# A decoder layer on one core: one step of a scan moved ahead of another, and row statistics of the next batch made during attention

## The chip, the cores and the metric

The kernel runs on one core of a Trainium2 chip. The core has five engines with a queue each, which meet only at semaphores: TensorE (PE; its weight loads are listed as PEld), VectorE (DVE), ScalarE (ACT), GpSimd (POOL), and SyncE (SP), which issues the DMAs. An engine works through its queue in order, and a wait holds up all that stands behind it. The metric is the device time of one execution in microseconds (us). The kernel before takes 4476.42 us (median of three runs, 4476.28 to 4478.08).

## The reference, cut to what matters

All is float32. The input x is 4 batches of 1024 rows of 512 numbers.

```
x = x + mamba_block(layernorm(x))                        # two scans, forward and backward
x = x + cross_attention(layernorm(x), ctx, ctx, mask)    # 16 heads of 32
x = x + moe_attention(layernorm(x))                      # 16 experts of 64

_mamba2:  z, xBC, dt = split(x @ in_proj_w.T)
          scan over rows:  h = h * dA_t + dt_t * x_t * B_t ;  y_t = h . C_t
          y = y + D * x ;  y = y * silu(z) ;  rmsnorm(y) @ out_proj_w.T
cross_attention:  Q, K, V = projections; softmax(Q K^T / sqrt(32), causal, masked) V @ W_o.T + b_o
layernorm:  (x - mean(row)) / sqrt(var(row) + 1e-5)
```

## The kernel before

Four stages follow one another with barriers between them: the forward scan (tiles named `mf_`), the backward scan (`mb_`), the cross attention (`xa_`) and the expert attention (`ff_`). In each stage a generator `order()` lists the steps, and every engine walks the same list and does its own part of each step. The list therefore sets the order within every engine's queue, SyncE's included; no planner stands behind it.

**The scans.** The rows are cut into 32 chunks of 128 (8 for each batch), and a loop counter n runs over slots. In slot n, `mixed` has TensorE make the gate projection z of chunk n+1 in two halves (line 1260) between the products within chunk n (L1241), and ScalarE the tanh of z (L833). `carry` has TensorE make the product of chunk n with the state that came from the chunk before (L1278, the inter-chunk product) and the state's increment (L1284); VectorE scales the first (L1078) and adds the second to the state (L1090). `gate` has VectorE finish silu(z) in two halves, reading z from PSUM (L1066); that frees the two PSUM banks `mf_proj`. In the forward scan the next user of these banks, in even slots up to 26, is `xT`: TensorE transposes two tiles of rows (L1173) for a later group of two chunks. After that come `output`, with the decay matrices (L1293, L1296; they need the bank that the state's increment was in) and the output product (L1309). In the list, `mixed`, `carry`, `gate` follow in this order in every slot; in even slots nothing of VectorE stands between `carry` and `gate`. Before them VectorE does the convolution taps (L940).

**The cross attention.** One batch after the other. `head()`: x of the batch is loaded in two halves of 1 MB into `src` (which also holds the exponentials of the attention, so the load waits for its last transposes); VectorE makes the row statistics of eight tiles of 128 rows (`stats`, one bn_stats each), per half the reciprocal root in a chain of 12 dependent small steps (`ln`), and normalizes the tiles (`xn`). `body()`: each tile is transposed by TensorE (`src` n), copied by ScalarE and split into a high and a low part by VectorE (L1823); eight `kq` steps make Q and K for four groups of four heads each, through DRAM, and `v` the values. Of these, the even ones need tiles 0 to 3 of the source, the odd ones tiles 4 to 7. The low part of the transposed source lies in the memory from which the output product `o` of the batch before reads, so VectorE's part of `src` 0 waits for the last `o`.

The attention proper is 32 tiles, 8 for each group g (i is the tile in the group, n = 8g + i). For each of four heads: scores (L1960, L1961), a row extreme on VectorE (`minima`, L1866), the exponential on ScalarE (L1781), transposes (L1967), copies on VectorE and ScalarE (L1874, L1790), products with V (L1983). After tiles 3 and 7 of a group VectorE scales the result (L1889, L1891), one tile later, and SyncE moves it (`scale`, L1692). At the end of tile 7 of groups 0 and 1, `loads` has SyncE issue the loads of Q and K for group g+2 (L1683): 4 heads, 2 halves, q and k, 3 parts, 48 DMAs of 64 KB.

```
                if now and now[1] == NT - 1 and now[0] + 2 < NHG:
                    yield from loads(now[0] + 2)
```

The eight output steps `o` t (projection on TensorE, residual and bias in the two buffers of `res`: SyncE loads x again (L1698), GpSimd adds the bias (L1728), VectorE adds the product (L1896), SyncE stores (L1705)) begin in the last tiles of a batch; six of them run at the boundary to the next batch, interleaved in the list with that batch's `head()`. `res` t can be loaded when the store of `res` t-2 has landed. Between the first group's result, which is staged in `res`, and `o` 0 these two buffers are unused.

Of the kernel before, what the change touches and what calls it, by code (L numbers as in the profile page):

```python
# [14 lines left out]
P = 128  # L15
# [86 lines left out]
def rsqrt(nc, step, out, x, v, a, scale, eps):  # L102


    step(nc.vector.tensor_scalar(v, x, scale, eps, ALU.mult, ALU.add))
    step(nc.vector.tensor_scalar(out.bitcast(I32), v.bitcast(I32), -0.5, RSQRT_SEED, ALU.mult, ALU.add))
    for _ in range(3):
        step(nc.vector.tensor_tensor(a, out, out, ALU.mult))
        step(nc.vector.scalar_tensor_tensor(a, a, -0.5, v, ALU.mult, ALU.mult))
        step(nc.vector.scalar_tensor_tensor(out, a, 1.5, out, ALU.add, ALU.mult))  # L110


def split_weight(nc, dve, stage, stage_loaded, hi_ready, half_ready, n, hi, lo):
# [153 lines left out]
def mamba_pass(nc, backward, x_in, w_in, conv_w, conv_b, dt_bias, a_log, d_skip, rms_w, w_out, w_proj,  # L267
# [17 lines left out]
    with ExitStack() as ctx:  # L285
# [122 lines left out]
        def order():  # L408

            yield "load", 0  # L410
            if not backward:
                yield "norm", 0
            for e in range(KD):
                yield "weights", e
                if e == 1:
                    yield "params", 0
            if backward:
                yield "load", 1
            yield "raw", 0
            yield "split", 0  # L420
            yield "split", 1
            if not backward:
                yield "xT", 0
                yield "load", 1
            yield "consts", 0
            for e in range(KD, 2 * KD):
                yield "weights", e
            yield "split", 2
            yield "split", 3
            for n in range(-3, N + 1):  # L430
                if not backward and n % 2 == 0 and 0 <= n // 2 + 2 < NGF:
# [24 lines left out]
                if 0 <= n - 1 < N:  # L456
                    yield "square", n - 1
                if n % 2 and 0 <= (n + 3) // 2 < NGF:
                    yield "tanh", (n + 3) // 2
                if -1 <= n < N:  # L460
                    yield "mixed", n
                if 0 <= n < N:
                    yield "carry", n
                if n % 2 and 0 <= (n + 3) // 2 < NGF:
                    yield "product", (n + 3) // 2
                if -1 <= n < N:
                    yield "gate", n
# [904 lines left out]
def cross_attention(nc, x_in, ctx_in, mask_in, wts, bq, bk, bv, bo, out):  # L1372
# [23 lines left out]
        return g * mine.count(mine[at]) + mine[:at].count(mine[at])  # L1396

    NV = sum(by_vector(t, n) for t in range(NT) for n in range(len(PACK[t])))
    kq_dram = [nc.dram_tensor(tag + n + "_dram", (2, D, S), F32).ap() for n in "kq"]
    held = []  # L1400
    with ExitStack() as ctx:
# [66 lines left out]
        resb_ready = sig("resb_ready", NT)  # L1468
        out_ready = sig("out_ready", NT)
        stored = [sig(f"stored{i}", NT // 2, 16) for i in range(2)]  # L1470
        dve_step = sig("dve_step", 2 * (2 + RSQRT_STEPS))
        const_ready, par_loaded, const_dve = sem("const_ready"), sem("par_loaded"), sem("const_dve")
        stage_loaded = [sem(f"stage_loaded{i}") for i in range(2)]
        hi_ready, half_ready, bq_ready = sem("hi_ready"), sem("half_ready"), sem("bq_ready")
# [13 lines left out]
        def loads(g):  # L1488
            for half in range(2):
                for h in range(g * HG, (g + 1) * HG):  # L1490
                    yield "load", (h, "q", half)
                    yield "load", (h, "k", half)

        def body():

# [14 lines left out]
            for n in range(len(TILES) + 1):  # L1510
# [42 lines left out]
                    yield from loads(1)  # L1553
                if now and now[0] == NHG - 1 and now[1] > QT + 1:
                    yield "o", now[1] - QT - 2
            yield "scale", scale.pop()

        def order():
# [10 lines left out]
            for it in range(B):  # L1569
                if it == 0:  # L1570
                    yield "split", 0, 0
                for what, n in body():
                    if it == 0 and what == "load_ctx":
                        yield "split", 0, 1
                        yield "fetch", 0, 2
# [8 lines left out]
                yield "load_x", it + 1, 1  # L1584
                yield "o", it, QT - 1
                yield "load_mask", it + 1, 0
                yield "o", it, QT
                ahead = [n for n in head() if n[0] != "load_x"]
                cut, end = ahead.index(("xn", 0)), ahead.index(("ln", 1)) + 1
                for what, n in ahead[:cut]:  # L1590
                    yield what, it + 1, n
                yield "o", it, QT + 1
                for what, n in ahead[cut:end]:
                    yield what, it + 1, n
                yield "o", it, QT + 2
                for what, n in ahead[end:]:
                    yield what, it + 1, n
                yield "o", it, QT + 3

        def run(batch):  # L1600
# [29 lines left out]

        @block.sync
        def _(sp):
            for s in ctx_loaded + x_loaded + [mask_loaded] + kq_stored + front_loaded + back_loaded + o_moved + res_loaded + stored:
                s.start(sp)
            for t, a in params:
                sp.dma_start(t, a).then_inc(par_loaded, 16)
# [7 lines left out]
            def batch(it):  # L1644
# [49 lines left out]
                def output(t):  # L1694
# [3 lines left out]
                        sp.dma_start(res[:, t % 2, :], x_in[it, t * P:(t + 1) * P, :]).then_inc(res_loaded[t % 2].sem, 16)  # L1698

                    if t == 0:  # L1700
                        load_res(0)
                    if t + 1 < NT:
                        load_res(t + 1)
                    sp.wait_ge(out_ready.sem, out_ready.at(it, t))
                    sp.dma_start(out[it, t * P:(t + 1) * P, :], res[:, t % 2, :]).then_inc(stored[t % 2].sem, 16)  # L1705

                return {"fetch": fetch, "load_mask": mask, "load_x": load_x, "load_ctx": load_ctx, "kq": store, "load": load, "scale": move,
                     "o": output}

            run(batch)  # L1710
# [84 lines left out]

        @block.vector
        def _(dve):
            for s in [mask_ready, xn_ready, slo_ready, kqlo_ready, v_ready, mx_ready, ptv_ready, rs_ready,
                      head_ready, sp_ready, out_ready, dve_step]:
                s.start(dve)  # L1800
            v_ = nc.vector
# [12 lines left out]
            def batch(it):  # L1814
# [14 lines left out]
                    v_.tensor_scalar(maskf, mask8, -NEG, None, ALU.mult).then_inc(mask_ready.sem, 1)  # L1829

                def stats(t):
                    dve.wait_ge(x_loaded[t // 4].sem, x_loaded[t // 4].at(it, 0))
                    if t == 0:
                        dve.wait_ge(xn_ready.sem, xn_ready.at(it, -1))
                    last = v_.bn_stats(stat[:, t, :], src[:, t, :])
                    if t % QT == QT - 1:
                        step(last)

                def norm_x(half):
                    mine = slice(half * QT, (half + 1) * QT)  # L1840
                    for t in range(half * QT, (half + 1) * QT):
                        last = v_.bn_aggr(mv[:, t, :], stat[:, t, :])
                    step(last)
                    rsqrt(nc, step, xr[:, mine], mv[:, mine, 1], tmp[:, 0, mine], tmp[:, 1, mine], 1.0, EPS)

                def normed(t):
                    x = src[:, t, :]
                    v_.tensor_scalar(x, x, mv[:, t, 0:1], xr[:, t:t + 1], ALU.subtract, ALU.mult).then_inc(xn_ready.sem, 1)

# [43 lines left out]
                def output(t):  # L1893
# [1 line left out]
                    dve.wait_ge(o_full.sem, o_full.at(it, t))  # L1895
                    v_.tensor_tensor(res[:, t % 2, :], gen["o", t][:], res[:, t % 2, :], ALU.add).then_inc(out_ready.sem, 1)  # L1896

                return {"split": split, "src": source, "mask": mask, "stats": stats, "ln": norm_x, "xn": normed, "kq": channels, "v": values,
                     "score": minima, "turn": turned, "recip": recip, "scale": scaled, "o": output}

            run(batch)
# [776 lines left out]
```

## Time and profile before

| | us |
|---|---|
| median of three runs | 4476.42 |
| the profiled execution | 4481.21 |
| its span, first to last instruction | 4479.5 |
| forward scan, about | 100 to 1110 |
| cross attention, about | 2240 to 3520 |
| TensorE busy over the span | 4064.1 (91%) |
| VectorE busy over the span | 3152.3 (70%) |
| mean granted TensorE clock | 0.961 |

An execution is one pass over the four stages. In the timeline a row is the start and length of one or several like instructions, engine, line of the kernel, operation, output and inputs; the bracket at its end gives the idle time of the engine ahead of it and who ended that. L12 is line 12 of the kernel. A busy share is over a stretch; a wait is put down to the one that came last.

### The profile page before, as it was taken

The numbers are of one execution on the slowest core, as the hardware profiler recorded it, in microseconds if no ns is written. First come the engines' busy times: TensorE is split into PE (matmuls) and PEld (weight loads), VectorE is DVE, ScalarE is ACT, GpSimd is POOL, SyncE is SP. The second block draws the span as 40 slices with busy tenths as digits, with TensorE's granted clock in tenths as the row PEclk, the third lists the DMA queues.
The fourth block names the chain that finished last, engine by engine and source line by source line (L and its number), as shares of the span: only waits on it lengthen the run. The fifth ranks groups of instructions, "written<-read, shape, count | busy, mean of one in ns | idle before, by whom it ended". The sixth has DMA issues, their size and how long they took to land. (4 is left out here: it accounts for less than half of the span.)

```text
span 4479.5 us, 71612 instructions
## 1 busy us (share of the span) xinstructions
PE 4064.1 (91%) x26200; PEld 3023.7 (68%) x26200; DVE 3152.3 (70%) x6457; ACT 1652.2 (37%) x3472; POOL 1034.0 (23%) x597
## 2 busy tenths in 40 slices
PE   6999999998799999999778888898898799999999
PEld 5767676765566666666466676576576478787877
DVE  5787878774489999899657647657557566666664
ACT  3434343432333333343237537447357311111111
POOL 0333434343055555555500000000000000000000
PEclk8999999999899999999889999999999899999999
DMA  2110111001201111111143142242341310101000
GB/s 107 37 37 29 38 42 39 28 35 39 86 26 51 44 39 45 51 44 37 40 175 100 62 142 84 92 134 62 117 126 50 121 34 24 34 22 36 27 26 19
DMA packets 150049, 266.40 MB, mean 59 GB/s; under 512 B 30276, under 2 KB 36424, under 8 KB 149704
## 3 DMA queue, kind: packets, MB, share of 16 engines
q1 hardware_dynamic: 149704, 261.83, 17.5%
q8 instruction: 213, 3.49, 0.3%
q14 instruction: 132, 1.08, 0.1%
HBM read 164.88 MB, written 88.34 MB: 57 GB/s over the span
## 5 line engine op out<-in xcount | busy, mean ns | idle before, releaser
L1866 DVE TENSOR_REDUCE xa_mn<-xa_s 128x1 f32<-128x896 f32 (+7 forms) x512 | 373.0, 751 | 135.8 <-PE xa_s L1961 134.8
L1781 ACT ACTIVATE xa_src<-xa_s,xa_mn 128x896 f32<-128x896 f32 (+7 forms) x512 | 377.7, 740 | 231.6 <-DVE xa_mn L1866 230.3
L1967 PE MATMUL xa_gen<-xa_ident,xa_src 128*128 128x128 f32 x2304 | 310.2, 278 | 53.3 <-ACT xa_pT L1790 26.3
L73 PE MATMUL ff_wb<-ff_w_hi,ff_st_hi 128*128 128x512 f32 x768 | 323.8, 422 | 10.4 <-DVE ff_parts L2472 10.4
L940 DVE SCALAR_TENSOR_TENSOR mb_cv<-mb_xc,mb_cw,mb_cv 128x256 f32<-128x256 f32 x432 | 310.8, 773 | 31.9 <-ACT mb_xc L746 27.8
L1728 POOL TENSOR_TENSOR xa_res<-xa_res,xa_bor 128x512 f32<-128x512 f32 x32 | 40.5, 1270 | 1244.7 <-DMA xa_res<-after_mamba_dram 1244.7
L74 PE MATMUL ff_wb<-ff_w_hi,ff_st_lo 128*128 128x512 f32 x768 | 311.9, 406 | 0.0
L75 PE MATMUL ff_wb<-ff_w_lo,ff_st_hi 128*128 128x512 f32 x768 | 311.1, 405 | 0.0
L1967 PEld LDWEIGHTS xa_gen<-xa_ident,xa_src 128*128 128x128 f32 x2304 | 251.1, 143 | 75.1 <-ACT xa_src L1781 59.5
L1309 PE MATMUL mb_ib<-mb_wc,mb_yT 128*128 128x512 f32 x512 | 262.6, 661 | 1.8 <-DVE mb_y L1078 1.0
L2240 POOL TENSOR_TENSOR ff_mixed<-ff_at,ff_rw 128x1024 f32<-128x1024 f32 x32 | 60.9, 1904 | 875.3 <-DVE ff_at L2500 875.3
L2472 DVE TENSOR_TENSOR ff_parts<-ff_wb,ff_rw 128x512 f32<-128x512 f32 x192 | 132.2, 688 | 156.9 <-PE ff_wb L75 156.5
L1309 PE MATMUL mf_ib<-mf_wc,mf_yT 128*128 128x512 f32 x512 | 236.1, 604 | 1.8 <-DVE mf_y L1078 1.0
L1874 DVE COPY xa_pT<-xa_gen 128x512 f32<-128x512 f32 (+3 forms) x352 | 183.5, 528 | 66.1 <-PE xa_gen L1967 63.6
L1790 ACT ACTIVATE xa_pT<-xa_gen 128x512 f32<-128x512 f32 x336 | 192.8, 587 | 98.0 <-PE xa_gen L1967 96.7
L1241 PEld LDWEIGHTS mf_yb<-mf_xdt,mf_decay 128*128 128x128 f32 x1024 | 191.4, 190 | 32.2 <-ACT mf_yT L818 1.4
L1241 PEld LDWEIGHTS mb_yb<-mb_xdt,mb_decay 128*128 128x128 f32 x1024 | 191.3, 189 | 31.4 <-ACT mb_yT L818 1.4
L1117 DVE TENSOR_TENSOR mb_decay<-mb_decay,mb_gb 128x512 f32<-128x512 f32 x128 | 201.9, 1581 | 1.0 <-ACT mb_decay L855 0.9
L940 DVE SCALAR_TENSOR_TENSOR mf_cv<-mf_xc,mf_cw,mf_cv 128x256 f32<-128x256 f32 x432 | 189.6, 476 | 1.1
L73 PE MATMUL mb_proj<-mb_xt_hi,mb_w_hi 128*128 128x256 f32 x576 | 169.0, 293 | 23.1 <-DVE mb_w_lo L870 21.8
L1309 PEld LDWEIGHTS mb_ib<-mb_wc,mb_yT 128*128 128x128 f32 x512 | 102.1, 209 | 128.1 <-issue 128.1
L1983 PE MATMUL xa_acc<-xa_pT,xa_vv 128*32 128x128 f32 x4608 | 156.0, 279 | 32.8 <-DVE xa_pT L1874 19.7
(494 smaller groups left out, 11031.7 us busy)
## 6 DMA issues: line engine op xcount, KB each, us to landing
xa_qa<-xa_q_dram SPq DMA_DIRECT2D x384, 64.0 KB, 2.0
xa_q_dram<-xa_kq SPq DMA_DIRECT2D x32, 512.0 KB, 2.8
xa_k_dram<-xa_kq SPq DMA_DIRECT2D x32, 512.0 KB, 2.8
xa_ka<-xa_k_dram SPq DMA_DIRECT2D x192, 64.0 KB, 2.0
xa_st<-xa_k_dram SPq DMA_DIRECT2D x192, 64.0 KB, 2.0
mf_xg<-in_x_dram SPq DMA_DIRECT2D x16, 512.0 KB, 5.1
turned_dram<-mf_xt_hi SPq DMA_DIRECT2D x16, 512.0 KB, 2.7
turned_dram<-mf_xt_lo SPq DMA_DIRECT2D x16, 512.0 KB, 4.0
```

The costliest lines, as they stand in the source:

```text
L73: nc.tensor.matmul(out, w_hi, x_hi, start=first, stop=False)
L74: nc.tensor.matmul(out, w_lo, x_hi, start=False, stop=False)
L75: return nc.tensor.matmul(out, w_hi, x_lo, start=False, stop=last)
L940: last = v_.scalar_tensor_tensor(cv[:, m, :], xc[:, m, o:o + GN], cw[:, m, j:j + 1], cv[:, m, :], ALU.mult, ALU.add)
L1117: v_.tensor_tensor(d, d, bcast(gb[:, c % 2, 0:P], 1, Q4), ALU.mult).then_inc(mix_ready.sem, 1)
L1241: last = mm(yb["y", c, h // 8][:, h % 8 * HP:(h % 8 + 1) * HP], decay[:, (NQ * c + q) % ER, h % Q4, :], xdt[:, c % 2, h * HP:(h + 1) * HP] ...
L1309: last = mm(ps[:], yT[:, k, :], wc[:, k, :], start=k == 0, stop=k == KI - 1)
L1781: a_.activation(pq[:, hh, 0:w], s1[g, i, hh][:, 0:w], ACT.Exp, scale=-1.0, bias=mn[:, i % 2, hh:hh + 1], accum_out=sums[:, i // QT, i % QT ...
L1790: a_.activation(pT[:, k, 0:w], gen["turn", g, i, k][:, 0:w], ACT.Copy).then_inc(pta_ready.sem, 1)
L1866: v_.tensor_reduce(mn[:, i % 2, hh:hh + 1], s1[g, i, hh][:, 0:(i + 1) * P], AX.X, ALU.min).then_inc(mx_ready.sem, 1)
L1874: v_.tensor_copy(pT[:, k, 0:w], gen["turn", g, i, k][:, 0:w]).then_inc(ptv_ready.sem, 1)
L1967: last = tr(ps[:, n * P:(n + 1) * P], pq[:, hh, j * P:(j + 1) * P], ident[:])
```

## The change

In the forward scan, `gate` of even slots stands ahead of `carry` in the list; odd slots and the backward scan keep their order.

In the cross attention, the row statistics of the next batch (batches 1 to 3) are made during the attention of the current one. A new step `peek` t has SyncE load tile t of the next batch's x into `res[t % 2]`, which is free then; it waits until `stats` t-2 has read the buffer. `stats` reads from there. A function `ahead` places them: two `peek` at tile n = 9, `stats` 0 to 7 at the end of tiles n = 13 to 20, each followed by the `peek` two tiles on, and three steps of the reciprocal-root chain at the end of each of tiles 21 to 28. At a tile's end they stand behind all else of this tile in the list, `loads` included. At the boundary, `xn` of the first half, `src` 0 and 1, `xn` of the second half, `src` 2 and 3 and the mask now stand between the output steps; the body of the next batch begins at `src` 4. In all 24 more DMAs of 256 KB.

```diff
                 if -1 <= n < N:
                     yield "mixed", n
+                if -1 <= n < N and not backward and n % 2 == 0:
+                    yield "gate", n
                 if 0 <= n < N:
                     yield "carry", n
...
-                if -1 <= n < N:
+                if -1 <= n < N and (backward or n % 2):
                     yield "gate", n
...
+    LN_STEPS = (1 + RSQRT_STEPS) // QT
+    AHEAD_SRC = QT
+    LAG = QT
...
+        def ahead(g, i):
+
+            n = g * NT + i - NT - 1
+            if n == 0:
+                yield "peek", 0
+                yield "peek", 1
+            t = n - LAG
+            if 0 <= t < NT:
+                yield "stats", t
+                if t + 2 < NT:
+                    yield "peek", t + 2
+            if NT <= t < 2 * NT:
+                for _ in range(LN_STEPS):
+                    yield "ln_step", (t - NT) // QT
...
                 if now and now[0] == NHG - 1 and now[1] > QT + 1:
                     yield "o", now[1] - QT - 2
+                if now:
+                    yield "ahead", now
...
                 yield "o", it, QT - 1
                 yield "load_mask", it + 1, 0
+                for t in range(QT):
+                    yield "xn", it + 1, t
                 yield "o", it, QT
...
+                yield "src", it + 1, 0
+                yield "src", it + 1, 1
+                for t in range(QT, NT):
+                    yield "xn", it + 1, t
                 yield "o", it, QT + 1
...
+                yield "src", it + 1, 2
+                yield "src", it + 1, 3
+                yield "mask", it + 1, 0
                 yield "o", it, QT + 2
...
+                def peek(t):
+                    sp.wait_ge(o_moved[t % 2].sem, o_moved[t % 2].at(it - 1, 0))
+                    if t >= 2:
+                        sp.wait_ge(stat_ready.sem, stat_ready.at(it, t - 2))
+                    sp.dma_start(res[:, t % 2, :], x_in[it, t * P:(t + 1) * P, :]).then_inc(peek_loaded[t % 2].sem, 16)
...
                 def stats(t):
-                    dve.wait_ge(x_loaded[t // 4].sem, x_loaded[t // 4].at(it, 0))
+                    if it:
+                        dve.wait_ge(peek_loaded[t % 2].sem, peek_loaded[t % 2].at(it - 1, t // 2))
+                    else:
+                        dve.wait_ge(x_loaded[t // 4].sem, x_loaded[t // 4].at(it, 0))
...
+                    x = res[:, t % 2, :] if it else src[:, t, :]
+                    v_.bn_stats(stat[:, t, :], x).then_inc(stat_ready.sem, 1)
```

## Rows read from the trace of the kernel before

**Rows 1.** Windows, forward scan: length, busy us (instructions) by engine, granted clock, DMA.
```profile
100.00:1110.00 1010.00, 964.94 (x5411) 694.88 (x5409) 775.29 (x1814) 388.27 (x780) 366.64 (x174) 0.99 0.10 33
```
**Rows 2.** Waits, forward scan: who waited for whom, total us, times, longest.
```profile
PE mf_proj L1173 <- DVE mf_zs L1066: 24.4, 14, 1.9
...
PE mf_dec L1293 <- DVE mf_state L1090: 10.4, 14, 0.7
```
**Rows 3.** Timeline of VectorE in one even slot.
```profile
440.61 6.27 DVE L940 SCALAR_TENSOR_TENSOR mf_cv<-mf_xc,mf_cw,mf_cv 128x256 f32<-128x256 f32 x15
448.67 1.29 DVE L1078 TENSOR_TENSOR mf_y<-mf_ib,mf_ecs 128x512 f32<-128x512 f32 x2 [1.79 <-PE mf_ib L1278]
...
450.64 1.27 DVE L1066 SCALAR_TENSOR_TENSOR mf_zs<-mf_zs,mf_proj 128x512 f32<-128x512 f32 x2
```
**Rows 4.** Timeline of ScalarE in the same slot.
```profile
447.51 0.60 ACT L833 ACTIVATE mf_zs<-mf_proj 128x512 f32<-128x512 f32 x1 [3.90 <-PE mf_proj L1260]
```
**Rows 5.** Timeline of TensorE in the same slot.
```profile
448.46 1.08 PE L1284 MATMUL mf_dec<-mf_xw,mf_gb 128*64 128x512 f32 x4
451.46 1.16 PE L1173 MATMUL mf_proj<-mf_ident,mf_xg 128*128 128x128 f32 x8 [1.92 <-DVE mf_zs L1066]
```
**Rows 6.** Timeline of SyncE's queue, batch 0: the first loads, the move behind the last.
```profile
2432.28 1.24 SPq L1683 DMA_DIRECT2D xa_qa<-xa_q_dram  x3
...
2456.93 0.47 SPq L1692 DMA_DIRECT2D xa_st<-xa_kq  x1
```
**Rows 7.** Timeline of VectorE, batch 0, tiles 17 and 18.
```profile
2443.61 0.69 DVE L1891 TENSOR_TENSOR xa_kq<-xa_acc,xa_kq 128x512 f32<-128x512 f32 x1
...
2446.18 1.02 DVE L1866 TENSOR_REDUCE xa_mn<-xa_s 128x1 f32<-128x384 f32 x2 [0.30 <-PE xa_s L1961]
```
**Rows 8.** Timeline, batches 1 and 2: VectorE at tile 18, SyncE's move.
```profile
2763.72 1.02 DVE L1866 TENSOR_REDUCE xa_mn<-xa_s 128x1 f32<-128x384 f32 x2 [0.30 <-PE xa_s L1961]
2775.67 4.94 SPq L1692 DMA_DIRECT2D xa_st<-xa_kq  x2
3079.02 1.02 DVE L1866 TENSOR_REDUCE xa_mn<-xa_s 128x1 f32<-128x384 f32 x2 [0.30 <-PE xa_s L1961]
3089.40 0.47 SPq L1692 DMA_DIRECT2D xa_st<-xa_kq  x1
```
**Rows 9.** Tile xa_res, whole trace: its DMAs' time from issue to landing.
```profile
DMA to landing us min/median/max: 2.0/2.6/6.4
```
**Rows 10.** DMA issues, 2432 to 2457 us: count, KB each, us to landing.
```profile
xa_st<-xa_kq SPq DMA_DIRECT2D x1, 256.0 KB, 4.1
```
**Rows 11.** Tiles xa_stat and xa_xr: count, ns min/median/max, first and last start.
```profile
L1835 DVE BATCH_NORM_STATS2 xa_stat<-xa_src x32: 667/675/694, 2246.3 to 3208.0; 128x6 f32<-128x512 f32 x32
...
L108 DVE TENSOR_TENSOR xa_tmp<-xa_xr x24: 161/161/1202, 2249.6 to 3211.7; 128x4 f32<-128x4 f32 x24
```
**Rows 12.** Timeline at the first batch boundary: TensorE, VectorE, GpSimd.
```profile
2548.05 20.87 PE L2004 MATMUL xa_gen<-xa_wo,xa_st 128*128 128x512 f32 x48
2558.30 0.69 DVE L1896 TENSOR_TENSOR xa_res<-xa_gen,xa_res 128x512 f32<-128x512 f32 x1 [5.74 <-POOL xa_res L1728]
2563.60 0.69 DVE L1896 TENSOR_TENSOR xa_res<-xa_gen,xa_res 128x512 f32<-128x512 f32 x1 [4.62 <-POOL xa_res L1728]
2569.12 1.27 POOL L1728 TENSOR_TENSOR xa_res<-xa_res,xa_bor 128x512 f32<-128x512 f32 x1 [2.29 <-DMA xa_res<-after_mamba_dram]
2582.66 3.65 PE L1919 MATMUL xa_s<-xa_ident,xa_src 128*128 128x128 f32 x16 [9.90 <-DVE xa_st L1823]
...
2590.70 0.75 DVE L1853 SCALAR_TENSOR_TENSOR xa_kq<-xa_gen,xa_bqc,xa_kq 128x512 fp32r<-128x512 f32 x1 [3.04 <-ACT xa_kq L1768]
```
**Rows 13.** Timeline at the second boundary: TensorE, VectorE.
```profile
2865.60 20.87 PE L2004 MATMUL xa_gen<-xa_wo,xa_st 128*128 128x512 f32 x48
...
2906.08 0.75 DVE L1853 SCALAR_TENSOR_TENSOR xa_kq<-xa_gen,xa_bqc,xa_kq 128x512 fp32r<-128x512 f32 x1 [2.15 <-ACT xa_kq L1768]
```
**Rows 14.** Windows, the transposes after that idle time at the first boundary.
```profile
2582.60:2586.00 3.40, 3.34 (x17) 3.37 (x17) 3.09 (x5) 1.70 (x3) 0.00 (x0) 0.50 0.84 286
```

More of the change, by code:

```diff
@@ L110, in rsqrt, with rsqrt_steps @@
         step(nc.vector.scalar_tensor_tensor(out, a, 1.5, out, ALU.add, ALU.mult))
+def rsqrt_steps(nc, step, out, x, v, a, scale, eps):
+    step(nc.vector.tensor_scalar(v, x, scale, eps, ALU.mult, ALU.add))
+    yield
+    step(nc.vector.tensor_scalar(out.bitcast(I32), v.bitcast(I32), -0.5, RSQRT_SEED, ALU.mult, ALU.add))
+    yield
+    for _ in range(3):
+        step(nc.vector.tensor_tensor(a, out, out, ALU.mult))
+        yield
+        step(nc.vector.scalar_tensor_tensor(a, a, -0.5, v, ALU.mult, ALU.mult))
+        yield
+        step(nc.vector.scalar_tensor_tensor(out, a, 1.5, out, ALU.add, ALU.mult))
+        yield
 def split_weight(nc, dve, stage, stage_loaded, hi_ready, half_ready, n, hi, lo):
@@ L1470, in cross_attention @@
         stored = [sig(f"stored{i}", NT // 2, 16) for i in range(2)]
-        dve_step = sig("dve_step", 2 * (2 + RSQRT_STEPS))
+        peek_loaded = [sig(f"peek_loaded{i}", NT // 2, 16) for i in range(2)]
+        stat_ready = sig("stat_ready", NT)
+        dve_step = sig("dve_step", 2 * (1 + RSQRT_STEPS))
         const_ready, par_loaded, const_dve = sem("const_ready"), sem("par_loaded"), sem("const_dve")
@@ L1572, in order @@
                 for what, n in body():
+                    if what == "ahead":
+                        if it + 1 < B:
+                            for what, n in ahead(*n):
+                                yield what, it + 1, n
+                        continue
+                    if it > 0 and what == "src" and n < AHEAD_SRC:
+                        continue
                     if it == 0 and what == "load_ctx":
@@ L1586, in order @@
                 yield "load_mask", it + 1, 0
+                for t in range(QT):
+                    yield "xn", it + 1, t
                 yield "o", it, QT
[L1588 to L1591, printed above, removed]
+                yield "src", it + 1, 0
+                yield "src", it + 1, 1
+                for t in range(QT, NT):
+                    yield "xn", it + 1, t
                 yield "o", it, QT + 1
-                for what, n in ahead[cut:end]:
-                    yield what, it + 1, n
+                yield "src", it + 1, 2
+                yield "src", it + 1, 3
+                yield "mask", it + 1, 0
                 yield "o", it, QT + 2
-                for what, n in ahead[end:]:
-                    yield what, it + 1, n
                 yield "o", it, QT + 3
@@ L1632, in _ @@
         def _(sp):
-            for s in ctx_loaded + x_loaded + [mask_loaded] + kq_stored + front_loaded + back_loaded + o_moved + res_loaded + stored:
+            for s in ctx_loaded + x_loaded + [mask_loaded] + kq_stored + front_loaded + back_loaded + o_moved + res_loaded + stored + peek_loaded:
                 s.start(sp)
@@ L1700, in output @@
                     if t == 0:
+                        if it + 1 < B:
+                            sp.wait_ge(stat_ready.sem, stat_ready.at(it + 1, NT - 1))
                         load_res(0)
@@ L1705, in output @@
                     sp.dma_start(out[it, t * P:(t + 1) * P, :], res[:, t % 2, :]).then_inc(stored[t % 2].sem, 16)
-                return {"fetch": fetch, "load_mask": mask, "load_x": load_x, "load_ctx": load_ctx, "kq": store, "load": load, "scale": move,
+                def peek(t):
[3 more added lines that the diff above has]
+                    sp.dma_start(res[:, t % 2, :], x_in[it, t * P:(t + 1) * P, :]).then_inc(peek_loaded[t % 2].sem, 16)
+                return {"peek": peek, "fetch": fetch, "load_mask": mask, "load_x": load_x, "load_ctx": load_ctx, "kq": store, "load": load, "scale": move,
                      "o": output}
@@ L1797, in _ @@
         def _(dve):
-            for s in [mask_ready, xn_ready, slo_ready, kqlo_ready, v_ready, mx_ready, ptv_ready, rs_ready,
+            for s in [mask_ready, xn_ready, slo_ready, kqlo_ready, v_ready, mx_ready, ptv_ready, rs_ready, stat_ready,
                       head_ready, sp_ready, out_ready, dve_step]:
@@ L1831, in stats, with norm_steps @@
                 def stats(t):
-                    dve.wait_ge(x_loaded[t // 4].sem, x_loaded[t // 4].at(it, 0))
+                    if it:
+                        dve.wait_ge(peek_loaded[t % 2].sem, peek_loaded[t % 2].at(it - 1, t // 2))
+                    else:
+                        dve.wait_ge(x_loaded[t // 4].sem, x_loaded[t // 4].at(it, 0))
                     if t == 0:
                         dve.wait_ge(xn_ready.sem, xn_ready.at(it, -1))
[L1835 to L1839, printed above, removed]
+                    x = res[:, t % 2, :] if it else src[:, t, :]
+                    v_.bn_stats(stat[:, t, :], x).then_inc(stat_ready.sem, 1)
+                def norm_steps(half):
                     mine = slice(half * QT, (half + 1) * QT)
+                    dve.wait_ge(stat_ready.sem, stat_ready.at(it, half * QT + QT - 1))
                     for t in range(half * QT, (half + 1) * QT):
@@ L1843, in norm_x, with norm_step @@
                     step(last)
-                    rsqrt(nc, step, xr[:, mine], mv[:, mine, 1], tmp[:, 0, mine], tmp[:, 1, mine], 1.0, EPS)
+                    yield
+                    yield from rsqrt_steps(nc, step, xr[:, mine], mv[:, mine, 1], tmp[:, 0, mine], tmp[:, 1, mine], 1.0, EPS)
+                def norm_x(half):
+                    for _ in norm_steps(half):
+                        pass
+                chains = {}
+                def norm_step(half):
+                    if half not in chains:
+                        chains[half] = norm_steps(half)
+                    next(chains[half])
                 def normed(t):
+                    dve.wait_ge(x_loaded[t // 4].sem, x_loaded[t // 4].at(it, 0))
                     x = src[:, t, :]
@@ L1896, in output @@
                     v_.tensor_tensor(res[:, t % 2, :], gen["o", t][:], res[:, t % 2, :], ALU.add).then_inc(out_ready.sem, 1)
-                return {"split": split, "src": source, "mask": mask, "stats": stats, "ln": norm_x, "xn": normed, "kq": channels, "v": values,
+                return {"split": split, "src": source, "mask": mask, "stats": stats, "ln": norm_x, "ln_step": norm_step, "xn": normed, "kq": channels, "v": values,
                      "score": minima, "turn": turned, "recip": recip, "scale": scaled, "o": output}
```

## The prediction

> **What bounds the kernel now.** The windows come first. In the forward scan TensorE is busy 964.94 of 1010 us at a granted clock of 0.99 [rows 1]: there, only what lets TensorE idle is worth time. So the waits of that stage come next: 14 times, 24.4 us in all, TensorE stands at the transposes of `xT` until VectorE's gate frees the bank, and 14 times, 10.4 us in all, at the decays until the state is added [rows 2]. Then one even slot in the timeline: TensorE is done with the state's increment at 449.54 and starts the transposes at 451.46 [rows 5]; VectorE meanwhile does the inter-chunk product, the state and then the gate [rows 3]. In the cross attention, no engine is full and the chain score, minimum, exponential, transpose sets the pace; VectorE stands in it at every head. So there the question is who holds up VectorE, and the view for it is the timeline of SyncE's queue beside VectorE's.
>
> **The gate ahead of the product.** Nothing is added. VectorE ends the taps at 446.88 (440.61 + 6.27) and waits 1.79 us for the product's matmul until 448.67 [rows 3]. The two gate halves take 1.27 us; the second needs the tanh that ends at 448.11 (447.51 + 0.60) [rows 4], so it runs from there to about 448.8, half a gate being 0.64. The product then starts at about 448.75 instead of 448.67: the wait that the gate fills costs 0.1 us more at most. The banks are free at 448.8, before TensorE needs them at 449.54. What is late next is the state: VectorE has it at about 450.8 as before, while the eight transposes, which now begin at 449.54 and take 1.16 us [rows 5], end near 450.7; the second decay matmul then waits 0.1 to 0.3 us. In the odd slots this wait is 0.74 us each (10.4 / 14) [rows 2]. So of 24.4 / 14 = 1.74 us a slot about 0.2 stays: 14 x 1.54 = 21.6 us gained. Bounds: 24.4 if nothing stays, 14.0 if the state's wait is as long as in the odd slots (14 x 1.0). Behind it VectorE and ScalarE run 1.2 to 1.5 us earlier too, and VectorE is busy 775 of 1010 us [rows 1], so I see nobody who would give it back.
>
> **The statistics, VectorE's part.** Eight bn_stats of 0.675 us and 24 small steps, 0.16 us each and some 0.2 with the wait for themselves [rows 11], go into 16 tile ends of each of three batches. VectorE idles there until the next tile's first score; before tile 18 it is 0.30 us [rows 7]. A step of 0.6 to 0.7 us in such a gap delays the minimum by some 0.35; beside the one below, of the 16 ends five (before tiles 2 to 4 of a group) are as narrow: 1.8 us a batch, 5 in all. I take 3. Bounds: 0 and 16 x 0.35 x 3 = 17.
>
> **The statistics, SyncE's part.** Every `peek` is a DMA on SyncE's queue. `peek` 4 is at the end of tile 15, and that is where the list also has the 48 loads of group 3, ahead of it. In batch 0 these are issued from 2432.28 to 2456.93: 24.65 us, 0.51 us each [rows 6]. The next thing in the queue, today, is the move of a result that VectorE had ready at 2444.30 (2443.61 + 0.69) [rows 7]; it went 12.6 us late, and nobody waited for it. In the changed kernel `peek` 4 stands in that place, and VectorE waits for it: `stats` 4 is at the end of tile 17, and VectorE comes there at 2445.88, the end of its work before the 0.30 us gap [rows 7]. Behind `stats` 4 in VectorE's queue stand the minima of tile 18, and for these wait the exponentials, the transposes and all that follows. The tile lands 2.6 us after the issue by this tile's median [rows 9], 4.1 by the move that stood there [rows 10]. Taking 2.6: landing 2459.5, statistics 0.675, so the first minimum of tile 18 at 2460.2 instead of 2446.18, 14.0 us late. Batch 1: 2775.67 + 3.3 - 2763.72 = 15.2. Batch 2: 3089.40 + 3.3 - 3079.02 = 13.7 [rows 8]. Together 42.9 us. During the stall TensorE can only make the scores of tile 18 and a few transposes ahead. After it, its clock will be low: after 9.90 us of idling [rows 12] the next 3.4 us ran at 0.50, the lower level of 1.2 GHz [rows 14]. At half rate, 3.4 us hold 1.7 us of work; beside the other engines I charge 1 us a stall: 46 us. Bounds: 3 x 1.7 and 3 x 1.5 (a landing of 4.1) more than 42.9, which is 52.5; 37 if TensorE's work ahead gives back 2 us a stall; and 0 if the queue were through in time. The other tiles come in time: SyncE is free at tiles 13 and 14, `peek` 5 stands right behind `peek` 4, and 6 and 7 follow the statistics that they wait for. The fourth batch has no successor and no stall.
>
> Of the issue time, the Trainium skill has a sentence that speaks for the change ("DMA: Bandwidth & Descriptors", section "Issuing engines are not separate DMA queues"): the time that a sequencer takes to initiate a DMA is usually small relative to the DMA itself. By it `peek` 4 would be out soon after 2432.28 and nothing would stall. The trace of this stretch doesn't agree: 0.51 us each, 48 in a row.
>
> **The batch boundary.** Gone are the statistics and chains of both halves; the work left is the same, in another order. I follow the first boundary from the first `o` at 2548.05 [rows 12]. TensorE: three `o` of 3.48 (20.87 / 6) to 2558.5; VectorE's `o` 3 ends at 2559.0, held by its residual as before, so `xn` 0 is ready at 2559.5 and the first transposes follow; with them and four tiles in all (0.5 each), the last `o` ends at about 2572.2. Only then may VectorE write its part of `src` 0. It does `src` 0 and 1 (0.6 each), four `xn` (0.53 each), `o` 5 to 2576.3, `src` 2 and 3, the mask, `o` 6 to 2578.8. `o` 7 needs a store, a load and GpSimd's add after `o` 5: from `o` 4's end (2564.29) to the end of the add two further on (2570.39) that chain is 6.1 us [rows 12]. So `o` 7 ends at 2583.1, and the four parts of `src` 4 to 7 at 2585.6: `kq` 1 starts there. Today it starts 0.9 us before VectorE's first `kq` part at 2590.70, at 2589.8: 4.1 us gained. At the second boundary this part stands 40.48 us behind the first `o`, against 42.65 at the first [rows 12, 13], so 1.9 us are gained; I take the third like the first. That is 10, and 2 less for `kq` 0 and 1, which run in pieces and partly at the low clock: 8. Bounds: 15, if `o` 7's chain is 1.5 us faster each time and the clock stays up; -3, if that chain takes 3 to 4 us more behind the context's loads.
>
> **The sum.** -21.6 - 8 + 3 + 46 = +19.4 us. The profiled execution took 4481.21, so the same execution would take 4500.6; it lies 4.8 above the median of the runs, 4476.42, and from that median the sum gives 4495.8. I predict 4496.
>
> **The rivals.** A change under 0.2%, some 9 us, can't be told from none here: 4467.5 to 4485.4 is the same.
>
> A: the queue is not late, and the kernel is faster. Mechanism: 0.51 us an issue is not SyncE's own pace but that of what it hands the loads to, and `peek` 4 finds the queue empty before VectorE reaches tile 17's end. It decides where the 48 loads take under 11 us (2445.88 - 2.6 - 2432.28). Against it: SyncE's rows run on without a gap, and the move behind them waited for them in all three batches [rows 6, 8]. Time: 4476.4 - 21.6 - 8 + 3 = 4450. The sentence of the skill above would have it so. 12%.
>
> B: the stall is there, but paid for: 37 us of stall without a price for the clock, gains at their best, 24.4 and 15. For it: TensorE and ScalarE go on for some us while VectorE stands. Against: the minima of tile 18 come back to back with nothing saved on VectorE. 37 - 39.4 + 1 puts it at 4475, and the half-way cases up to 4485: the same. 14%.
>
> C: the stall, and the gains do not come: the gate's bank is free, but the state's wait takes its place (14 x 1.0 gained is the nearest row's bound; beyond it, 5), and at the boundary the chain of `o` 7 eats the statistics' time: 46 + 6 - 5 - 0 = +47, 4523. For it: VectorE's state is as late as today. Against: it is 0.1 to 0.3 us behind the transposes, not 1.7. 9%.
>
> The forecast itself, +10 to +36: 65%. Range, 8 times in 10: 4474 to 4512. That leaves out A and the outer half of C. Faster 0.13, the same 0.15, slower 0.72.
>
> **What would show it.** Right, if TensorE's waits for the gate at L1173 are gone from the scan and its waits for the state grow by 2 to 4 us; if VectorE's longest idle times in the attention are three of 12 to 15 us ahead of bn_stats, ended by the DMA into `xa_res`, and SyncE issues that DMA right after 48 loads; if `kq` 1 starts 2 to 4 us earlier after the first `o` of a boundary. Wrong, if that bn_stats starts without a wait (then A), or if TensorE's wait at L1173 only moves to L1293.

## The result and the profile after

The changed kernel takes 4497.57 us, median of four runs (4494.30 to 4499.15); the kernel before took 4477.25 beside it (four runs, 4476.28 to 4478.09). The ratio is 1.0042, 95% interval 1.0027 to 1.0057: slower by 20 us. The profiled span is 4495.7 us against 4479.5, so +16.2.

The forward scan first. The first fence has TensorE's waits there (who waited for whom, total us, times, longest), the second VectorE in one even slot, the third TensorE and the fourth ScalarE in that slot.

```profile
PE mf_dec L1310 <- DVE mf_state L1107: 10.7, 15, 0.8
PE mf_proj L1190 <- DVE mf_zs L1083: 3.4, 3, 1.1
```
```profile
429.66 6.27 DVE L957 SCALAR_TENSOR_TENSOR mf_cv<-mf_xc,mf_cw,mf_cv 128x256 f32<-128x256 f32 x15
435.96 0.69 DVE L1083 SCALAR_TENSOR_TENSOR mf_zs<-mf_zs,mf_proj 128x512 f32<-128x512 f32 x1
437.18 0.69 DVE L1083 SCALAR_TENSOR_TENSOR mf_zs<-mf_zs,mf_proj 128x512 f32<-128x512 f32 x1 [0.53 <-ACT mf_zs L850]
438.06 1.29 DVE L1095 TENSOR_TENSOR mf_y<-mf_ib,mf_ecs 128x512 f32<-128x512 f32 x2 [0.19 <-issue]
```
```profile
437.50 1.08 PE L1301 MATMUL mf_dec<-mf_xw,mf_gb 128*64 128x512 f32 x4
438.51 1.09 PE L1190 MATMUL mf_proj<-mf_ident,mf_xg 128*128 128x128 f32 x8
...
440.00 0.39 PE L1310 MATMUL mf_dec<-mf_later,mf_ident_b 128*128 128x512 bf16 x1 [0.18 <-DVE mf_state L1107]
```
```profile
436.55 0.60 ACT L850 ACTIVATE mf_zs<-mf_proj 128x512 f32<-128x512 f32 x1 [3.90 <-PE mf_proj L1277]
```

The gate now stands between the taps and the product, its second half waits 0.53 us for the tanh, and the transposes at L1190 follow the increment without the 1.92 us of before [rows 5]. The wait for the gate fell from 24.4 us to 3.4, that for the state stayed: 10.4 before [rows 2], 10.7 now. The slot shown is the only even one in which the state's wait (0.18 us) comes behind. The three waits for the gate that are left, 1.1 us each, stand in slots 8, 16 and 24, where a batch begins and there is no inter-chunk product.

Then batch 0 at tiles 15 to 18: SyncE's queue (SPq; 48 loads at L1730, then the peeks at L1760), and VectorE.

```profile
2406.08 1.25 SPq L1730 DMA_DIRECT2D xa_qa<-xa_q_dram  x3
...
2429.53 1.35 SPq L1730 DMA_DIRECT2D xa_st<-xa_k_dram  x3
2430.98 0.85 SPq L1760 DMA_DIRECT2D xa_res<-after_mamba_dram  x2
```
```profile
2418.95 0.74 DVE L1937 TENSOR_REDUCE xa_mn<-xa_s 128x1 f32<-128x256 f32 x2
2433.61 0.69 DVE L1894 BATCH_NORM_STATS2 xa_stat<-xa_res 128x6 f32<-128x512 f32 x1 [13.92 <-DMA xa_res<-after_mamba_dram]
2434.22 1.00 DVE L1937 TENSOR_REDUCE xa_mn<-xa_s 128x1 f32<-128x384 f32 x2
```

VectorE is ready for `stats` 4 at 2419.69, but `peek` 4 goes out at 2430.98, behind the last load, and lands 2.6 us later. Over the whole trace this happens three times; the next fence, of the waits ahead of tile xa_stat, gives the sum. The one behind it has windows of the first stall (columns as in [rows 1]).

```profile
DVE xa_stat L1894 <- DMA xa_res<-after_mamba_dram: 41.6, 3, 14.4
```
```profile
2423.00:2433.00 10.00, 0.17 (x2) 0.00 (x0) 0.00 (x0) 0.00 (x0) 0.00 (x0) 0.67 0.55 149
...
2436.00:2440.00 4.00, 3.99 (x28) 2.96 (x29) 2.86 (x6) 2.80 (x9) 0.00 (x0) 0.50 0.36 110
2440.00:2446.00 6.00, 5.59 (x58) 4.35 (x57) 5.21 (x9) 4.84 (x12) 0.00 (x0) 0.97 0.01 1
```

For some 10 us hardly any engine computes. Afterwards TensorE runs at a granted clock of 0.50, the level of 1.2 GHz, until about 2440. (It stood at 0.50 from 2420 to 2423 too, ahead of the idle stretch.)

Last, the first boundary, whose first `o` starts at 2538.07: VectorE, then one row of ScalarE, then one row of VectorE in the kernel before.

```profile
2552.27 0.69 DVE L1967 TENSOR_TENSOR xa_res<-xa_gen,xa_res 128x512 f32<-128x512 f32 x1 [1.45 <-POOL xa_res L1783]
2561.83 1.29 DVE L1878 TENSOR_TENSOR xa_st<-xa_s,xa_st 128x512 fp32r<-128x512 f32 x2 [8.87 <-PE xa_gen L2075]
...
2571.67 0.69 DVE L1967 TENSOR_TENSOR xa_res<-xa_gen,xa_res 128x512 f32<-128x512 f32 x1 [3.50 <-POOL xa_res L1783]
2572.28 2.47 DVE L1878 TENSOR_TENSOR xa_st<-xa_s,xa_st 128x512 fp32r<-128x512 f32 x4
...
2578.64 0.75 DVE L1924 SCALAR_TENSOR_TENSOR xa_kq<-xa_gen,xa_bqc,xa_kq 128x512 fp32r<-128x512 f32 x1 [3.23 <-ACT xa_kq L1823]
```
```profile
2583.33 0.69 ACT L1823 ACTIVATE xa_kq<-xa_gen,xa_bqc 128x512 fp32r<-128x512 f32 x1 [4.72 <-DMA xa_q_dram<-xa_kq]
```
```profile
2593.51 0.75 DVE L1853 SCALAR_TENSOR_TENSOR xa_kq<-xa_gen,xa_bqc,xa_kq 128x512 fp32r<-128x512 f32 x1 [2.06 <-ACT xa_kq L1768]
```

VectorE's part of `kq` 1 is at 2578.64, 40.57 us after the first `o`; before, it was at 2593.51, 45.46 us after it (the 42.65 of [rows 12] is the part of `kq` 0). There is a wait that was not there before: 8.87 us of VectorE at `src` 0 for the last output product. And ScalarE waits 4.72 us at `kq` 2 for the store of `kq` 0, issued right behind the context's loads; before, its longest wait for such a store at this boundary was 2.72.

To see where time goes, I cut each profile at fixed instructions: the forward scan from the first to the last inter-chunk product; the 32 reciprocals of the attention (one at the end of tiles 3 and 7 of each group). "Tile 18" is the sum, over batches 0 to 2, of the stretch between reciprocals that holds it; "boundaries" runs from a batch's last reciprocal to the next one's first; "last" from the last reciprocal to the end of the span. All in us; the kernels below the second line are the experiments. One of the six runs of peek_pool, at 5043.67 us and a granted clock of 0.784 where its others show 0.962 to 0.965, was slow and is left out of its times.

| | forward scan | tile 18 | other tiles, batches 0 to 2 | boundaries | last | span |
|---|---|---|---|---|---|---|
| before | 927.5 | 57.4 | 504.6 | 391.6 | 982.1 | 4479.5 |
| after | 908.0 | 103.6 | 503.5 | 381.7 | 985.4 | 4495.7 |
| gate_only | 907.9 | 56.3 | 503.3 | 393.3 | 981.0 | 4453.9 |
| rows_only | 927.5 | 104.2 | 506.1 | 384.1 | 976.0 | 4509.3 |
| peek4_first | 907.8 | 101.6 | 505.8 | 383.6 | 982.0 | 4493.6 |
| loads_halved | 907.9 | 168.4 | 504.7 | 385.7 | 985.3 | 4564.8 |
| peek_pool | 907.9 | 57.6 | 504.4 | 385.8 | 981.2 | 4450.2 |
| late_loads | 907.9 | 57.6 | 505.8 | 386.1 | 985.4 | 4456.9 |
| edge_order | 907.9 | 59.8 | 503.4 | 357.2 | 982.0 | 4420.3 |
| edge_both | 907.9 | 56.5 | 505.8 | 365.3 | 978.8 | 4434.3 |

After less before: -19.5 in the forward scan, +46.2 at tile 18, -1.1 in the other tiles, -9.9 at the boundaries. The remaining 0.5 of the 16.2 is not the change's: the scan's first product is 5.0 us earlier (156.0 against 161.0, but 156.9 in rows_only, whose scan is that of before), and the untouched stretches (backward scan and first head, batch 3, last stage) add 5.5. The last stage, the same code in every kernel, took 976.0 to 985.4: a difference of a few us in the total says nothing, one in a column may.

### The profile page after: what moved, and what is told of

Read it like the earlier page. It is cut to its first block and busy times, and to the rows that moved or that the text cites. A ratio compares the mean times of both kernels' runs of the same rounds, so it can differ in the third digit from the quotient of the medians.

```text
span 4495.7 us, 71662 instructions
## 1 busy us (share of the span) xinstructions
PE 4067.3 (90%) x26200; PEld 3023.4 (67%) x26200; DVE 3161.0 (70%) x6457; ACT 1652.6 (37%) x3472; POOL 1037.2 (23%) x597
## 5 line engine op out<-in xcount | busy, mean ns | idle before, releaser
L2038 PEld LDWEIGHTS xa_gen<-xa_ident,xa_src 128*128 128x128 f32 x2304 | 255.1, 144 | 75.6 <-ACT xa_src L1836 59.8
L1845 ACT ACTIVATE xa_pT<-xa_gen 128x512 f32<-128x512 f32 x336 | 192.9, 587 | 101.6 <-PE xa_gen L2038 100.1
```

The lines of the kernel that those rows point to most:

```text
L1845: a_.activation(pT[:, k, 0:w], gen["turn", g, i, k][:, 0:w], ACT.Copy).then_inc(pta_ready.sem, 1)
L2038: last = tr(ps[:, n * P:(n + 1) * P], pq[:, hh, j * P:(j + 1) * P], ident[:])
```

## The experiments

The first four ran on one chip beside the kernel before at 4478.95 (9 runs, 4472.02 to 4480.42), the last four beside it at 4477.46 (11 runs).

**gate_only** is the kernel before with the gate's part of the change alone.

```
+                if -1 <= n < N and not backward and n % 2 == 0:
+                    yield "gate", n
...
-                if -1 <= n < N:
+                if -1 <= n < N and (backward or n % 2):
                     yield "gate", n
```


> The kernel before with the first edit alone: the gate of even slots ahead of the inter-chunk product; the cross attention is as before. My theory: the forward scan is 24 to 25 us shorter, as in the trace of the changed kernel (first row statistics at 2221.6 against 2246.3), and nothing gives it back: 4477.3 - 24.7 = 4453, 4451 to 4455. Rival (the gain of the scan is an accident of this profile, or is lost in the stages behind): 4460 or more.

4455.65 us (five runs, 4447.91 to 4458.89), ratio 0.995 (0.9936 to 0.9963). The gain is real and stays: -23.3, a little short of the expectation. The table says why: the 24.7 that I took held the 5.0 us of the early start; the scan itself gained 19.6, the same in all eight kernels that have the edit, within 0.1.

**rows_only** is the change without that part.

> The changed kernel with the gate's place undone: only the row statistics move. If the two edits add up, the attention with its stalls costs 4497.6 - 4477.3 + 24.7 = +45, so 4522 (4518 to 4526), with three idle times of VectorE of 13 to 15 us ahead of bn_stats. Rival: the stall is partly an effect of the earlier start of the attention and is smaller here: under 4512.

4514.04 us (four runs, 4507.83 to 4519.18), ratio 1.0082 (1.0068 to 1.0096): +35.1, and three waits of 40.8 us in all. Below the 4518 that I expected, above the rival's 4512 by 2. Again the 24.7 was too large: with 19.5 the two edits add up to 4517 (4497.6 + 19.5), inside the range of its runs. The stall is as long as in the changed kernel, 104.2 against 103.6, so it does not depend on the earlier start.

**peek4_first** swaps two steps in the list:

```
+                if now:
+                    yield "ahead", now
                 if now and now[1] == NT - 1 and now[0] + 2 < NHG:
                     yield from loads(now[0] + 2)
```


> The changed kernel with the step ahead of the 48 loads at a tile's end, instead of behind them. Nothing else: the same DMAs, the same bytes. My theory (the place in SyncE's queue makes the stall): the peek of tile 4 goes out in time and statistics 4 wait for nothing; the peek of tile 5, a tile later in the list, now stands behind the 48 loads (24.65 us), and statistics 5 at the end of tile 18 wait instead. Tile 18 takes VectorE some 5 us, so three waits of 8 to 11 us stay of the three of 13 to 14.4: 4497.6 - 3 x 5 = 4483 (4478 to 4489). Rival 1 (the loads' bytes fill the DMA engines and the tile lands late wherever its issue stands): statistics 4 still wait 10 us or more, 4495 or more. Rival 2 (the stall is overlapped by other work and costs little): no change, 4495 to 4500.

4492.63 us (five runs, 4491.74 to 4500.30), ratio 1.0039 (1.0027 to 1.0052). `stats` 4 no longer waits; `stats` 5 does, as I said, but for 38.8 us in all, not for 24 to 33. SyncE's queue shows what I left out:

```profile
2392.89 16.31 SPq L1760 DMA_DIRECT2D xa_res<-after_mamba_dram  x3
2409.29 1.31 SPq L1730 DMA_DIRECT2D xa_qa<-xa_q_dram  x3
...
2433.77 0.37 SPq L1760 DMA_DIRECT2D xa_res<-after_mamba_dram  x1
```
```profile
2408.12 0.68 DVE L1894 BATCH_NORM_STATS2 xa_stat<-xa_res 128x6 f32<-128x512 f32 x1
...
2436.66 0.69 DVE L1894 BATCH_NORM_STATS2 xa_stat<-xa_res 128x6 f32<-128x512 f32 x1 [13.31 <-DMA xa_res<-after_mamba_dram]
```

`peek` 4 waits in SyncE's queue for `stats` 2 (2408.12 + 0.68), and behind it now stand the loads: they start at 2409.29 instead of 2406.08. The step that moved ahead took its own wait with it, and the loads behind it start 3.2 us later. By time alone this run lies between my 4489 and the rivals' 4495; which statistics wait, and the queue's rows, decide for the queue.

**late_loads** issues group 3's loads at the end of tile 20, behind `ahead`:

```
-                if now and now[1] == NT - 1 and now[0] + 2 < NHG:
-                    yield from loads(now[0] + 2)
+                if now == (0, NT - 1):
+                    yield from loads(2)
...
+                if now == (2, QT):
+                    yield from loads(3)
```


> The changed kernel with the 48 loads of group 3 issued at the end of tile 20 instead of tile 15; they are first needed at tile 24. By then all eight peeks are out. My theory: no idle time of VectorE at the statistics; the stall of 41.6 us and the low clock behind it go, 4497.6 - 43 = 4454 to 4455 at least if statistics in narrow gaps cost nothing (4447 to 4458), with 4444 the lower end if the boundary's whole gain of 8 shows. Two things could speak against it: the results' moves behind the loads at tile 20, for which nobody waits before tile 28, and the loads' own landing before tile 24, some 36 us later. Rival 1 (bytes, not queue): the stall moves to tile 24 and the time stays over 4485. Rival 2 (the cost is the extra VectorE work in the attention): 4480 or more without any long wait.

4458.67 us (five runs, 4447.37 to 4462.01), ratio 0.9951 (0.9938 to 0.9965). No statistics of a later batch wait, and tile 18 is back at 57.6. That is 39 us less than the changed kernel, 0.7 above my range, and neither the bytes nor VectorE's extra work makes the loss. Against gate_only it is 3.0 more with ranges that overlap: what the moved statistics are worth without the stall can't be read from these times.

**peek_pool** leaves the loads and lets GpSimd issue the peeks on its own queue (`g_.dma_start` with the same two waits).

> The changed kernel with the peeks issued by GpSimd on its own queue; SyncE's 48 loads stay at the end of tile 15, ahead of them in the list. My theory (only the shared queue makes the stall): the peeks pass the loads, no statistics wait for long, and the time is that of the kernel with the late loads, 4458.7 (4449 to 4464, as wide as its own runs lay). Rival (48 loads of 64 KB in flight hold up a transfer that is issued among them): the statistics of tiles 4 and 5 wait some us each, 4468 or more.

4453.94 us (five runs, 4451.95 to 4462.31), ratio 0.9951 (0.9939 to 0.9963). The peeks land 3.3 us after their issue, in the midst of the 48 loads (DMA issues of 2400 to 2440 us: count, KB each, median us to landing), and nothing waits for them:

```profile
xa_qa<-xa_q_dram SPq DMA_DIRECT2D x24, 64.0 KB, 2.1
xa_st<-xa_k_dram SPq DMA_DIRECT2D x24, 64.0 KB, 2.1
xa_res<-after_mamba_dram POOLq DMA_DIRECT2D x5, 256.0 KB, 3.3
```

The same loads stand at the same place and the stall is gone: its cause is the shared queue.

**loads_halved** cuts each of these 48 DMAs into two over the columns.

> The changed kernel with each of group 3's 48 loads of 64 KB cut into two of 32 KB: 96 issues, the same bytes, in the same place ahead of peek 4. If the queue's time goes by the number of DMAs (0.51 us each), peek 4 goes out 24.6 us later still and each of the three stalls grows from 13.9 to about 38: 4497.6 + 74 = 4571 (4555 to 4580). If it goes by bytes (128 KB in 1 us), nothing changes: 4495 to 4502. In between, the stalls' growth divided by 48 gives the price of one more DMA.

4564.83 us (four runs, 4561.28 to 4569.04), ratio 1.0194 (1.018 to 1.0209). The waits ahead of tile xa_stat, and SyncE's queue:

```profile
DVE xa_stat L1898 <- DMA xa_res<-after_mamba_dram: 107.2, 3, 35.8
```
```profile
2406.40 2.73 SPq L1732 DMA_DIRECT2D xa_qa<-xa_q_dram  x6
...
2450.08 2.74 SPq L1732 DMA_DIRECT2D xa_st<-xa_k_dram  x6
2452.93 1.11 SPq L1764 DMA_DIRECT2D xa_res<-after_mamba_dram  x2
```

The queue goes by the number of DMAs, not by bytes: (107.2 - 41.6) / 3 / 48 = 0.456 us for one more, and the rows say the same, 2.74 / 6. The two `peek` behind them in the changed kernel, 256 KB each, took 0.85 us together (2430.98). My 0.51 for each held a few slower issues (2.56 and 2.80 us for three, twice among the sixteen in the queue after) that the additional DMAs do not repeat; so +67 instead of +74.

**edge_order** goes after the 8.9 us at the boundary. It is late_loads with `xn` 4 to 7, `o` 5 and `o` 6 ahead of `src` 0:

```
                 yield "o", it, QT
-                yield "src", it + 1, 0
-                yield "src", it + 1, 1
                 for t in range(QT, NT):
                     yield "xn", it + 1, t
                 yield "o", it, QT + 1
-                yield "src", it + 1, 2
-                yield "src", it + 1, 3
+                yield "o", it, QT + 2
+                for t in range(AHEAD_SRC):
+                    yield "src", it + 1, t
                 yield "mask", it + 1, 0
-                yield "o", it, QT + 2
                 yield "o", it, QT + 3
```


> The kernel with the late loads, and at a batch boundary the list in another order: xn 4 to 7, o 5 and o 6 ahead of src 0, so that VectorE does them while it waits for the last output product (8.9 us idle three times ahead of src 0). Theory 1 (that wait and the chain of o 7 behind it set the start of kq 1): o 5 ends some 8 us earlier on VectorE, o 7 at about 26.8 us after the first o instead of 34 (2558.7 - 2524.75), kq 1 starts 7 us earlier, and three boundaries give 21: 4458.7 - 21 = 4438 (4430 to 4446). Rival (something else sets the start of kq 1, such as the loads of the context behind SyncE's last store): under 2 us a boundary, 4452 or more.

4422.68 us (four runs, 4416.04 to 4426.71), ratio 0.9876 (0.9863 to 0.9889): the fastest here, and 7 below the range that I gave. It is 36 less than late_loads, of which 28.9 are at the boundaries and the rest spread over stretches that are the same. VectorE at the first boundary:

```profile
2536.93 1.91 DVE L1919 TENSOR_SCALAR xa_src<-xa_src,xa_mv,xa_xr 128x512 f32<-128x512 f32 x4
2540.01 0.69 DVE L1967 TENSOR_TENSOR xa_res<-xa_gen,xa_res 128x512 f32<-128x512 f32 x1 [1.16 <-POOL xa_res L1783]
2543.25 0.69 DVE L1967 TENSOR_TENSOR xa_res<-xa_gen,xa_res 128x512 f32<-128x512 f32 x1 [2.55 <-POOL xa_res L1783]
2544.14 2.48 DVE L1878 TENSOR_TENSOR xa_st<-xa_s,xa_st 128x512 fp32r<-128x512 f32 x4 [0.20 <-PE xa_gen L2075]
...
2547.37 0.69 DVE L1967 TENSOR_TENSOR xa_res<-xa_gen,xa_res 128x512 f32<-128x512 f32 x1
```

The wait at `src` 0 is 0.20, and `o` 7 is 28.8 us behind the batch's last reciprocal (2518.54) instead of 36.9 in late_loads. That is 8.1, where I had 7; the boundaries gained 9.6 each. The other 1.5 go with the clock, which the windows show (late_loads first, then edge_order):

```profile
2553.00:2567.00 14.00, 11.65 (x35) 9.00 (x36) 5.70 (x9) 2.35 (x4) 1.27 (x1) 0.68 0.65 199
```
```profile
2550.00:2560.00 10.00, 9.69 (x42) 7.67 (x42) 2.44 (x4) 2.06 (x3) 0.00 (x0) 1.00 0.90 309
```

TensorE is busy for 28.12 of the 29 us before the first `kq` steps, against 24.72 of 29 in late_loads, and they run at the level of 2.4 GHz. That the clock makes the whole of the 1.5 was not tried by itself.

**edge_both** moves the context's two loads of 1 MB behind the stores of `kq` 0 and 1.

> The same, and the loads of the context behind the stores of kq 0 and 1 in SyncE's queue instead of ahead of them. In the changed kernel ScalarE waits up to 4.7 us at kq 2 and kq 4 for the landing of such a store beside the context's 2 MB. Theory: TensorE works through the eight kq steps without a gap meanwhile, so that wait is covered: no difference from the kernel without this edit within 3 us. Rival: the wait is on the path, three boundaries at 3 us, 9 us faster.

4436.60 us (four runs, 4432.47 to 4442.79), ratio 0.991 (0.9897 to 0.9923): 14 more than edge_order, where I expected no difference. Two reasons, both in the traces. In the first batch the list has the splitting of the next weights beside this load, and it moved too, to between `kq` 1 and 2: VectorE comes to its part of `kq` 2 late, TensorE waits 7.66 us for it at `kq` 5, and the first reciprocal is 10.0 us later (2341.3 against 2331.3). At the boundaries it costs 8.1 in all. ScalarE's longest wait for a store of `kq` at the first boundary, edge_order first, then edge_both:

```profile
2558.79 0.69 ACT L1823 ACTIVATE xa_kq<-xa_gen,xa_bqc 128x512 fp32r<-128x512 f32 x1 [4.49 <-DMA xa_q_dram<-xa_kq]
```
```profile
2577.51 0.69 ACT L1824 ACTIVATE xa_kq<-xa_gen,xa_bqc 128x512 fp32r<-128x512 f32 x1 [7.82 <-DMA xa_q_dram<-xa_kq]
```

The stores issued right behind the 2 MB land late: `kq` 0 and 1 after 7.0 and 4.9 us in edge_order, `kq` 2 and 3 after 9.7 and 8.2 in edge_both, where the median of these stores is 2.8. In edge_order the wait of 4.49 us is covered: from `kq` 1 to 7 VectorE takes 16.86 us (2554.34 to 2571.20), 2.81 a step, which is TensorE's own pace. The wait of 7.82, two steps later, is longer than that cover: 19.84 us for the same six steps. The longest waits at the other two boundaries are 6.4 and 3.4 us against 6.7 and 8.3, and over all three these steps take 7.8 us more, nearly the whole of the 8.1.

## Why the prediction was right, and where it was off

The forecast was 4496, the time 4497.57, and the terms of the sum came out one by one:

- The gate: -21.6 predicted, -19.5 measured, in all kernels that have it. The steps of the slot are as worked out: the product is held up a little (2.13 us behind the taps, 1.79 before), the transposes start with the increment's end, the second decay matmul waits 0.18 us. But I took that slot for all fourteen. In ten of them nothing stays, and in the three at the start of a batch 1.1 us each do: there is no product for the gate to go ahead of. And the waits for the state, which I had growing by 2 to 4 us, hardly grew: 10.4 before and 10.7 after; 14.9 in rows_only, whose scan is that of before, and 15.5 in gate_only, whose scan is the changed one. Gate and state together, the waits fell by 20.7; why the scan gained 1.2 less was not traced.
- VectorE's extra steps: +3 predicted. Over the eight kernels with moved statistics against the two without, the other tiles give +1.0; tile 18, over the four of the eight that have no stall, gives another +1.0. That is +2, about as much as such segments vary.
- The stall: +46 predicted, +46.2 measured. The idle time is 41.6; with 3 x 0.69 for the statistics, and without the 3 x 0.30 that VectorE stood idle there before [rows 7, 8], tile 18 starts 42.8 later in all, where I had 42.9. The issue rate, the landing (2.6) and VectorE's arrival, all read from the trace of before, hold in the changed kernel. What is left of the 46.2, 3.4, fits the 1 us a stall that I charged for the low clock; the windows show that clock, but no run shows its price by itself.
- The boundary: -8 predicted, -9.9 in this profile; the six kernels with the change's order average 384.5 against 392.5 for the two with the old, -8.0. No run has the statistics gone and the old order, so the two are one term here. The chain of `o` 7 sets the end as worked out: TensorE starts `kq` 1 at 36.7 us behind the first `o` (2574.81), where I had 37.6. That is 5.0, 2.6 and 5.5 us earlier than before at the three boundaries, more than my 2 to 4 at two of them, and the boundaries are 4.5, 2.5 and 2.9 shorter. So 3.2 of the 13.1 is lost behind the start of `kq` 1, most of it, 2.6, at the third boundary, where TensorE makes `kq` 1 at a granted clock of 0.53 (3233.3 to 3239.5, after 3.61 us of idling); I had taken off 2 for this. My text had VectorE wait there for the last `o` without calling it a loss: 8.9 us, which another order fills.

With the averages over kernels where there are any, the columns add up to -19.5 - 8.0 + 1.0 + 46.2 = +19.7; in the two profiles alone they give +15.7, and the medians differ by 20.3. So the terms bear the forecast out, but that it came within 2 us of the time is in part luck.

Rival A needed a queue that is free in time, and it was late by 11 us. Rival B needed the neighbours to work on: for 10 us none did. C needed the gains to fail, and both came. So the change is two gains of 19.5 and 8 and one loss of 46. The loss is no price of moving the statistics: peek_pool and late_loads have the statistics moved and no stall. The sentence of the Trainium skill in "DMA: Bandwidth & Descriptors", section "Issuing engines are not separate DMA queues", that the time to initiate a DMA is usually small relative to the DMA itself, does not carry this case: for one of these loads the issue is about a quarter of the 1.9 us to its landing, and 48 in a row hold the queue for 24.9 us (2406.08 to 2430.98); cutting them in two adds to it.

## What to carry to other kernels

A DMA that an engine waits for is as late as the queue that it stands in; so count the issues ahead of it in the list, at their measured pace, and move the burst that nobody needs yet. A step that is put ahead of others takes its own waits along and delays them all. And when work leaves a boundary, look which wait ends last there afterwards: an order that puts ready work into it was worth more here (28.9 us) than the change had gained at the boundaries (8).

## What the runs showed of the hardware that I had not expected

- An issue of these loads on SyncE's queue costs about 0.46 us at 32 KB as at 64 KB, and one of a `peek` of 256 KB no more (0.85 us for two); on GpSimd's queue it took 0.54 us for 256 KB.
- The first store of `kq` (512 KB) issued behind 2 MB of loads landed after 5.3 to 10.3 us in edge_order and edge_both, against a median of 2.8, and held ScalarE back by 3.4 to 8.3 us.
- The same stretch of code between two reciprocals mostly takes one of two lengths about 1.1 us apart (18.8 or 19.9, 30.6 or 31.6), in every kernel and without a pattern that I could find; what makes it stays open.
